# Layer norm of the next quarter ahead of the second matmul of this one, and a third buffer for the W1 tiles, in the feed-forward stages

## What is computed

```
x = x + mamba(layernorm(x))       # W_in, conv, selective scan, W_out
x = x + ffn(layernorm(x))         # "FFN a"
x = x + block_attention(layernorm(x))
x = x + ffn(layernorm(x))         # "FFN b", same weights

def ffn(x, W1, b1, W2, b2, scale):            # H = 4096, D = 1024
    lt = x[:, 1:17, :]; even = lt[:, ::2]; odd = lt[:, 1::2]
    m1 = (even[:, :4, :, None] * odd[:, :4, None, :]).reshape(B, H, D)
    m2 = (even[:, 4:, :, None] * odd[:, 4:, None, :]).reshape(B, D, H)
    h = x @ W1.T + scale * einsum('bsd,bhd->bsh', x, m1) + b1
    h = gelu(h)
    return h @ W2.T + scale * einsum('bsh,boh->bso', h, m2) + b2
```

## Time and profile before

| | |
|---|---|
| runs of the kernel before | 6078.03 and 6021.37 us, median 6049.7 |
| the profiled execution | 6021.37 us, span of its slowest core (core 3) 6019.8 us |
| spans of the cores in it | 5880.0 to 6019.8 us |
| TensorE matmul busy | 2887.0 us (48%), 12960 matmuls |
| VectorE busy | 2547.3 us (42%) |
| ScalarE busy | 1755.3 us (29%) |
| GpSimd busy | 397.9 us (7%) |
| DMA | 345.40 MB, mean 57 GB/s |

### The profile page before, as it was taken

How to read it: one execution, slowest core, us unless ns; L and a number is a source line. 1 busy time by engine, 2 the same in 40 slices (tenths; PEclk the granted TensorE clock), 3 DMA queues, 4 the chain that set the end, 5 groups by cost and what they waited for, 6 DMA issues and landing times.

```text
span 6019.8 us, 41620 instructions; the slowest of 8 cores (5880.0 to 6019.8 us)
## 1 busy us (share of the span) xinstructions
PE 2887.0 (48%) x12960; PEld 1231.0 (20%) x12960; DVE 2547.3 (42%) x2198; ACT 1755.3 (29%) x2562; POOL 397.9 (7%) x378
## 2 busy tenths in 40 slices
PE   4342334223432233322223248678764553778778
PEld 3211111011110111100001123233222232223223
DVE  0008998189981899729993000010112222010010
ACT  2214554055540555405551231201101221110210
POOL 1130111001110011100000100000000000000000
PEclk9976666666676666766566558778776665977878
DMA  7421000400005000040003832211232113221221
GB/s 119 91 45 32 18 21 15 101 28 18 21 15 108 22 20 20 15 100 11 13 11 88 161 135 63 77 53 60 71 83 64 55 57 106 64 67 56 67 67 56
DMA packets 202301, 345.40 MB, mean 57 GB/s; under 512 B 49924, under 2 KB 86916, under 8 KB 201060
## 3 DMA queue, kind: packets, MB, share of 16 engines
q1 hardware_dynamic: 173990, 289.47, 16.6%
q0 software_dynamic: 28096, 53.27, 5.3%
HBM read 301.06 MB, written 71.45 MB: 62 GB/s over the span
## 4 chain that ended last, share of the span: by engine, by line
PE 30%; DVE 26%; DMA 13%; issue 11%; DVEq 7%; ACT 6%; SPq 4%; POOL 2%; another core or an unknown queue 1%; ACTq 0%; POOLq 0%
DVE m_hall L57 14%; PE f_pAa L57 9%; PE f_pAb L57 9%; DVEq L73 7%; DVE m_dBall L57 5%; SPq L57 4%; PE a_pA L57 4%; PE m_pB L57 3%; DMA f_w1a<-s_W1T 2%; DMA f_w1b<-s_W1T 2%; DVE m_txd L57 2%; DMA m_yfr<-s_yfc 2%; DMA p_wnat<-W 1%; DMA xres<-x 1%; PE m_pA L57 1%
## 5 line engine op out<-in xcount | busy, mean ns | idle before, releaser
L57 DVE TENSOR_TENSOR_SCAN m_hall<-m_dA,carry,m_dBall 128x512 bf16<-128x512 f32 x1024 | 1342.6, 1384 | 12.0 <-issue 11.0
L57 PE MATMUL m_pB<-m_gall,eye 128*128 128x512 bf16 x1024 | 364.4, 534 | 1431.0 <-DVE m_gall L57 1431.0
L57 ACT ACTIVATE m_dA<-m_delta,A_fm 128x512 f32<-128x512 f32 x1024 | 731.9, 721 | 949.4 <-DVE m_hall L57 854.0
L57 ACT ACT_TABLE_LOAD x158 | 202.7, 1283 | 1371.2 <-DVE tmp L57 815.9
L57 PEld LDWEIGHTS m_pB<-m_gall,eye 128*128 128x128 bf16 x1024 | 127.2, 129 | 1656.8 <-issue 1627.8
L57 DVE TENSOR_TENSOR f_txa<-xres,b_bc 128x1024 f32<-128x1024 f32 x16 | 19.6, 1225 | 814.9 <-PE f_pAa L57 814.9
L57 DVE TENSOR_TENSOR f_txb<-xres,b_bc 128x1024 f32<-128x1024 f32 x16 | 19.6, 1225 | 809.2 <-PE f_pAb L57 809.2
L57 POOL TENSOR_TENSOR m_diag<-convw_fm,eye 128x1920 bf16<-128x1920 f32 x64 | 238.8, 3732 | 1421.0 <-PE m_pB L57 1421.0
L57 DVE BATCH_NORM_STATS2 stat<-xres 128x6 f32<-128x512 f32 x128 | 82.1, 683 | 575.8 <-DMA xres<-s_x 353.4
L57 PE MATMUL f_pAa<-f_xna,f_w1a 128*128 128x512 bf16 x1024 | 274.6, 417 | 72.2 <-DMA f_w1a<-s_W1T 66.1
L57 PE MATMUL f_pAb<-f_xnb,f_w1b 128*128 128x512 bf16 x1024 | 270.3, 412 | 72.8 <-DMA f_w1b<-s_W1T 64.2
(11 more groups left out here) (154 smaller groups left out, 3472.2 us busy)
## 6 DMA issues: line engine op xcount, KB each, us to landing
xres<-s_x SPq DMA_DIRECT2D x96, 512.0 KB, 3.3
f_w1a<-s_W1T SPq DMA_DIRECT2D x128, 256.0 KB, 2.6
f_w1b<-s_W1T SPq DMA_DIRECT2D x128, 256.0 KB, 2.6
s_x<-xres SPq DMA_DIRECT2D x48, 512.0 KB
xres<-x SPq DMA_DIRECT2D x32, 512.0 KB, 3.7
m_wz<-s_WinT POOLq DMA_DIRECT2D x64, 256.0 KB, 2.9
m_wzz<-s_WinT SPq DMA_DIRECT2D x64, 256.0 KB, 2.7
m_wouta<-s_WoutT SPq DMA_DIRECT2D x64, 256.0 KB, 2.6
```

The costliest lines, as they stand in the source:

```text
L57: box["i"] = getattr(e, fname)(*a, **kw)
```

## The change

`emit_ffn` alone is edited. `f_xn` gets two buffers, the layer norm gets a PSUM tile of its own (`f_pLN`), and `f_w1` gets a third buffer with a semaphore of its own (`s_wzz[0]`). The layer norm of quarter 0 is emitted ahead of the loop. That of quarter h+1 is emitted inside the loop of quarter h, behind mm1 and ahead of mm2; quarter 3 has none. TensorE waits for the layer norm of its quarter by a count remembered in `lntok`. The load of W1 chunk c waits for the matmuls of chunk c-3 (`s_q3` at the count in `W1TOK`) and no longer for a gelu; the first three loads of a quarter wait for nothing of their own.

```diff
-            xn_fm = fb("f_xn" + tag, [128, 8, THF], BF16)
+            xn_fm = fb("f_xn" + tag, [128, 2, 8, THF], BF16)
-            w1s = fb("f_w1" + tag, [128, 2, 1024], BF16)
+            w1s = fb("f_w1" + tag, [128, 3, 1024], BF16)
...
-            lnps_bf = pA[:, 0, :].bitcast(BF16)[:, 0:1024]
+            pLN = fs.enter_context(nc.psum_tensor("f_pLN" + tag, [128, 1024], BF16))
...
+            W1TOK = {}
+            w1sem = (s_wzp[0], s_wzp[1], s_wzz[0])
+            l_ev = emit_ln(s_x, list(range(NTHF)), xn_fm[:, 0, :, :], "plain", pLN[:, :])
+            lntok = {0: l_ev.n}
             for h in range(4):
-                tiles = list(range(h * NTHF, (h + 1) * NTHF))
-                l_ev = emit_ln(s_x, tiles, xn_fm, "plain", lnps_bf)
-                te.wait(l_ev, l_ev.n)
+                xh = xn_fm[:, h % 2, :, :]
+                te.wait(l_ev, lntok[h])
                 if h == 0:
-                    ve.wait(l_ev, l_ev.n)
-                    ve.tensor_copy(out=ltc[:, :, :], in_=xn_fm[:, :, 1:17]).inc(l_lt, 1)
+                    ve.wait(l_ev, lntok[0])
+                    ve.tensor_copy(out=ltc[:, :, :], in_=xh[:, :, 1:17]).inc(l_lt, 1)
...
-                te.wait(l_ev if h == 0 else l_ev)
...
                 for c in range(32):
                     sl = c % 2
-                    if c >= 2:
-                        sy.wait(l_h, l_h.n - 1)
-                    sy.dma_start(out=w1s[:, sl, :], in_=s_W1T[c, :, :]).inc(s_wzp[sl], 16)
-                    te.wait(s_wzp[sl])
+                    sl3 = c % 3
+                    if c >= 3:
+                        sy.wait(s_q3, W1TOK[c - 3])
+                    sy.dma_start(out=w1s[:, sl3, :], in_=s_W1T[c, :, :]).inc(w1sem[sl3], 16)
+                    te.wait(w1sem[sl3])
                     if c >= 2:
                         te.wait(l_h, l_h.n - 1)
...
                     tok.inc(s_q3, 1)
+                    W1TOK[c] = s_q3.n
...
+                if h < 3:
+                    l_ev = emit_ln(s_x, list(range((h + 1) * NTHF, (h + 2) * NTHF)),
+                                   xn_fm[:, (h + 1) % 2, :, :], "plain", pLN[:, :])
+                    lntok[h + 1] = l_ev.n
                 te.wait(l_h, l_h.n)
                 te.wait(lg, lg.n)
                 for tt in range(NTHF):
```

More of the change, by code:

```diff
@@ L885, in emit_ffn @@
                                         lhsT=ltc[:, k, 1:8:2],
-                                        rhs=xn_fm[:, k, t0:t0 + tw],
+                                        rhs=xh[:, k, t0:t0 + tw],
                                         start=(k == 0), stop=(k == 7))
@@ L908, in emit_ffn @@
                             tok = te.matmul(out=pA[:, sl, t0:t0 + tw],
-                                            lhsT=w1s[:, sl, k * 128:(k + 1) * 128],
-                                            rhs=xn_fm[:, k, t0:t0 + tw],
+                                            lhsT=w1s[:, sl3, k * 128:(k + 1) * 128],
+                                            rhs=xh[:, k, t0:t0 + tw],
                                             start=(k == 0), stop=False)
```

## The result

| | before | after |
|---|---|---|
| median of all runs | 6013.0 us (13 runs) | 5782.1 us (14 runs) |
| lowest, highest | 5920.7, 6078.0 | 5637.4, 5864.9 |
| the profiled execution | 6021.4 | 5783.6 |

The ratio is 0.9461, with a 95% interval of 0.9394 to 0.9528: 5.4% faster. The forecast was 5860 against 6049.7, so 0.969, or 3.1% faster, from terms that add up to 174 us.

The account below looks back on a forecast made before the run. TensorE's queue was taken to bound both FFNs, waiting for the layer norm and W1 tiles. Terms -147 + 63 + 14 - 110 + 6 = -174 gave 5847 from the profiled 6021.4, 5876 from the median; predicted 5860, range 5765 to 5940.

Parts of the forecast that it names:

- A: Between mm2 and the next mm1: layer norm gone, W1 load behind the store remains; six turns 186.4 to 40 us, -147.
- the far bound: Turn from mm2 to mm1: a W1 load behind stores taking 7.98 us, putting mm1 at t + 11.6 instead of 6.6.
- B: Between mm1 and mm2: layer norm moved, only its start hidden; mm2 about 15 us behind the last v block, +63.
- C: In mm1: W1 loaded three chunks ahead, matmuls gapless at clock 0.81, 94.7 us per mm1; 770 against 880, -110.
- at full clock: Bound on the mm1 saving from loading W1 earlier, if gapless matmuls are granted 1.00: -231.
- half-clock start: First mm2 tile behind the layer norm slower by 2.4 us, +14 for six; in mm1 after the turn, 7 in all.
- D: First tiles of mm2 in three quarters lose speed inherited from gapped mm1: five tiles by 1.1 us, +6.
- full-clock rival: mm1 stays at 1.00 although dense, because row matmuls and v blocks give it breath: 5740 to 5745; chance 0.14.
- The other rivals: mm1: gain given back as clock 5937, chance 0.13; third buffer does nothing 5970, 0.08; slower clock 6270, 0.04.
- half-clock stretch behind each v block: Rival in mm1: gain of C given back as clock, +77 to 5937; chance 0.13.

Follow-up runs that it names:

- e6: Kernel after, with the next quarter's layer norm emitted tile by tile inside mm2 instead of as a block ahead of it: ratio to before 0.9368.
- e1: Kernel before with only the third W1 buffer and the wait for the matmuls of chunk c-3; layer norm left where it was: ratio 0.9634.
- e11: Control: the kernel after, unchanged, run again on the chip of e10: ratio to before 0.9507, median 5677.0 us.
- e10: Kernel after with e6, e8, a later wait for f_vfl and three W1 tiles loaded ahead of mm2: ratio to before 0.9246, median 5516.1 us.
- e2: Kernel after with two W1 buffers and the old gelu wait, so only the layer norm's move remains: ratio 0.9856.
- e3: Kernel after with mm1's 32 single-row matmuls per quarter left out and v blocks after the last chunk: mm1 687 to 694 us in sum without 0.81.
- e4: Kernel after with mm2's 16 single-row matmuls per tile spread singly, one behind every fourth large matmul: ratio 0.9590.
- e8: Kernel after with mm2's 16 single-row matmuls per tile in groups of four, one group per sixteen large matmuls: ratio 0.9479.

## Why the prediction was right and where it was wrong

**A** (-147) was right: 41 us of turns where 40 were forecast. The load behind the store took 3.28 us (the far bound, 7.98, was in the earlier trace rows), near the low end that was taken. (That low end adds up to 6.1 us by its own terms, 2.77 + 0.32 + 0.3 + 2.74, and not to 5.9; the 6.6 that was used doesn't hang on it.) The wait that takes the place of the layer norm is the one named.

**B** (+63) was right: 98 us of gaps against 99, with the first transpose 4.0 us behind the v block where 3.25 was forecast, and mm2 about 15 behind it. e6 shows it from the other side.

**C** (-110) was the step that failed. Its mechanism held: the W1 waits are gone outside the turns, the v blocks keep their 0.93 us. Its size was taken from the wrong clock. Measured are -147 on core 2, which was at 0.81 for a part of the time, and -191 on core 5, which was not, against -110; the bound "at full clock" (given as -231, by its own terms -110 - 117 = -227) was for core 3, which would have had to leave its 0.81 as well. e1 and e11 show 83 us per mm1 on all cores in place of 94.7. The two prices themselves held: 95 to 97 us at 0.81 for 94.7, and 83 at full clock for 80.1, where some 3 us of each quarter are the half-clock start that was costed at 7 in all. What was wrong is which of them was taken.

The sentence that failed is "gapless matmuls on all cores are what mm2 is, and mm2 is granted 0.81". Two readings in it were wrong.

- The earlier trace rows were read as 263 ns per matmul, a clock of 0.81. On core 1 that average was a mixture. Its weight loads in the kernel before show a start at half clock, one load every 0.43 us, and then 49 loads in 10.46 us, 0.21 us each, which is full clock:

```profile
3976.20 0.15 PEld L57 LDWEIGHTS f_pAa<-f_w2a,f_ha 128*128 128x128 bf16 x1 [0.28 <-issue]
3976.63 0.15 PEld L57 LDWEIGHTS f_pAa<-f_w2a,f_ha 128*128 128x128 bf16 x1 [0.28 <-issue]
3977.06 0.15 PEld L57 LDWEIGHTS f_pAa<-f_w2a,f_ha 128*128 128x128 bf16 x1 [0.28 <-issue]
3977.38 10.46 PEld L57 LDWEIGHTS f_pAa<-f_w2a,f_ha 128*128 128x128 bf16 x49 [0.17 <-issue]
```

  The same holds for the 0.81 of the second window in the earlier trace rows: its clock records are at 1.00 and 0.50 up to 3959 us and at 0.81 and 0.50 behind it.
- Core 3 did have stretches at a true 0.81, but the earlier trace rows show one of them in mm1 with its gaps: 3823.54 to 3826.10, a chunk in 2.56 us, in a part where TensorE still waits for every second tile. The row that priced the dense mm1 was itself not dense, which spoke against the reading and was passed over. A look at the same stretch on cores 0 and 1, at 1.00, would have shown that 0.81 was not what the code brings on.

The Trainium skill's rule on three busy cores of a die (TensorE: Matmul & The Clock Gate, on the HAM clock gate), which the prediction set beside this step, doesn't hold here as stated: in e1, e10 and e11 all eight cores run dense matmuls in both FFNs, and no core has a record at 0.81. The value 13/16 does appear (0.81) in other executions, in dense and in gapped code, but on two cores of a die while the other two can be at 1.00. What brings it on was not found.

**D** (+6) rested on the same reading and falls with it. The **half-clock start** of mm2 (+14) was seen but cost nothing new: the first tile of mm2 takes 19.5 to 19.8 us behind the layer norm (e11, quarters 0 to 2, mean of the cores) and 19.7 to 20.2 in the kernel before (tiles without 0.81), where it already had more half clock in it, 4.6 to 5.9 us against 3.7 to 4.3. mm2 in sum went from 640 on core 1 to 627 on core 5, while 20 more were forecast. Over tiles without any 0.81 the means of all cores give 642 before and 626 in e11, and the half-clock time in a quarter's mm2 is 24 us before and 18.5 in e11. So what fell is time at half clock, most of it in the second tile. Why it fell was not tested; e1 and e2, each with one part of the change, lie at 627 to 644.

In total: the 174 us forecast were 230 on a core with 0.81 and 287 on one without. The full-clock rival (0.14) had the right clock; its 5740 to 5745 stands beside 5724 by the ratio. Its reason, that row matmuls and v blocks keep the clock up, is not borne out: e3 has none among its chunks and is granted 1.00. The row that was given against it, mm2's clock, was the misread one. The other rivals are refuted by e1: part C alone is worth 3.7%, and its mm1 of 83 us leaves no room for a half-clock stretch behind each v block.

## What to carry to other kernels

Before a duration is taken as "the clock of dense code", look at the spacing of single instructions inside it and at another core: a mean of full and half clock looks just like a third level. When a layer norm or another vector stage is moved off one boundary, ask which engine queue it still stands in: ahead of mm2 only its start was hidden, and the rest only once it was placed where TensorE had matmuls of its own to run between its tiles. A load that waits for the consumer of a result, where the last reader of its buffer would do, gives away the whole of that consumer's time: here half of the gain of prefetching was in the wait and needed no buffer.

## What the runs showed of the hardware that was not expected

- Sixteen single-row matmuls in a row (3.78 us, TensorE busy all the time) are mostly followed by a half-clock stretch of over 3 us in the next tile: in e11 in 31 of 64 second tiles of a quarter and in 126 of 128 third and fourth ones. The same sixteen singly (e4) or in four groups of four (e8, e10) are not, in none of 192 tiles each. By quarter, mm2 is granted 0.83 to 0.93 in e11 and 1.00 in e10.
- A single-row matmul of 256 columns costs 0.23 us in a block of 16, 0.28 in a group of four (4.56 us less sixteen large ones of 0.216, by four), and 0.42 alone between matmuls of 128 rows.
- The granted clock of 0.81 comes in dense and in gapped code alike, on two neighbouring cores at a time, for stretches within an execution. The other two cores of the same die can be at 1.00 meanwhile (before, 3823 to 3863 us: 1.00, 1.00, 0.81, 0.81).
